# A transformer layer rewritten as one program, interleaved by batch

## The reference

```python
mod = (_silu(L0_c) @ L0_wmod).reshape(L0_c.shape[0], 6, 1, -1)
sa, ca, ga, sb, cb, gb = (mod[:, 0], ..., mod[:, 5])
ga = (2 * (ga >= 0) - 1) * jnp.maximum(jnp.abs(ga), 0.25)   # gb likewise
h = _layernorm(x, axis=-1) * (1 + ca) + sa
x = x + ga * _L0_attn_ref(h, ...)
h = _layernorm(x, axis=-1) * (1 + cb) + sb
x = x + gb * _L0_ffn_ref(h, ...)
```

## Time and profile before

| | us |
|---|---|
| median of three runs | 2005.65 |
| lowest, highest | 1998.06, 2006.18 |
| the profiled execution | 2002.72 |
| its span in the trace | 2000.9 |
| PE, DVE, ACT, POOL busy in the span | 1893.9, 1251.0, 1113.4, 486.1 |
| granted clock, mean | 0.967 |

### The profile page before, as it was taken

One profiled execution on the slowest core, in us unless ns is written; L12 is line 12 of the kernel. 1 busy time (PEld: TensorE's weight loads), 2 busy tenths in 40 slices (PEclk: granted clock), 3 DMA queues, 4 the chain that ended last, 5 costly groups with the idle time before them and its releaser, 6 DMA issues. The chain is left out here.

```text
span 2000.9 us, 30064 instructions
## 1 busy us (share of the span) xinstructions
PE 1893.9 (95%) x9271; PEld 1575.8 (79%) x9271; DVE 1251.0 (63%) x2969; ACT 1113.4 (56%) x2582; POOL 486.1 (24%) x466
## 2 busy tenths in 40 slices
PE   7769589999999999999999999999999967999999
PEld 3557278888888888888888888888888856788887
DVE  5864856666666766666676666666666636643534
ACT  3344356666666666666566666666656625523423
POOL 0620643324132240313413123131221111010010
PEclk8669789999999999999999999999999978999999
DMA  9100245655656555465654545546454455211010
GB/s 363 44 1 1 84 141 157 192 165 169 186 154 189 154 164 158 145 203 180 207 162 152 178 123 170 157 147 181 118 176 134 145 160 164 80 53 53 16 58 21
DMA packets 170380, 275.30 MB, mean 138 GB/s; under 512 B 18744, under 2 KB 111928, under 8 KB 170304
## 3 DMA queue, kind: packets, MB, share of 16 engines
q1 hardware_dynamic: 167760, 270.18, 43.7%
q10 hardware_dynamic: 2544, 4.19, 0.7%
HBM read 173.65 MB, written 100.66 MB: 137 GB/s over the span
## 5 line engine op out<-in xcount | busy, mean ns | idle before, releaser
L1526 DVE CUSTOM_DVE_ANT_0 ps<-ps,mask 128x512 f32<-128x512 f32 (+3 forms) x512 | 236.2, 522 | 339.2 <-PE ps L1250 339.0
L1211 PE MATMUL ps<-hA,wq 128*128 128x512 f32 x1536 | 386.0, 400 | 0.9 <-DVE qT L1511 0.8
L1283 PE MATMUL ps<-wo,oT 128*128 128x512 f32 x1536 | 372.8, 394 | 3.0 <-issue 1.6
L1416 ACT ACTIVATE pt<-pd 128x1280 fp32r<-128x1280 f32 x128 | 163.2, 1275 | 353.4 <-PE ps L1265 340.4
L1283 PEld LDWEIGHTS ps<-wo,oT 128*128 128x128 f32 x1536 | 287.9, 189 | 62.6 <-issue 1.8
L1211 PEld LDWEIGHTS ps<-hA,wq 128*128 128x128 f32 x1536 | 279.0, 188 | 57.9 <-issue 0.9
L1397 ACT ACTIVATE probs<-ps,nmax 128x512 f32<-128x512 f32 (+3 forms) x512 | 262.8, 532 | 47.9 <-DVE nmax L1526 47.9
L1265 PE MATMUL ps<-pt,V 128*128 128x512 f32 (+2 forms) x1152 | 252.9, 349 | 18.3 <-DVE pt L1550 18.3
L1405 ACT ACTIVATE probs<-probs,rinv 128x512 f32<-128x512 f32 (+3 forms) x512 | 246.2, 552 | 31.3 <-DVE rinv L1532 31.3
L1265 PEld LDWEIGHTS ps<-pt,V 128*128 128x128 f32 x1152 | 196.8, 190 | 45.7 <-issue 21.2
L1250 PE MATMUL ps<-kT,qT 128*128 128x512 f32 (+2 forms) x1152 | 225.3, 340 | 0.0
(11 more groups left out here) (205 smaller groups left out, 2623.6 us busy)
## 6 DMA issues: line engine op xcount, KB each, us to landing
turned_blocks<-tp SPq DMA_DIRECT2D x128, 640.0 KB, 2.9
pd<-turned_blocks SPq DMA_DIRECT2D x512, 160.0 KB, 3.3
wq_in<-in_L_attn_w_q_dram SPq DMA_DIRECT2D x16, 1024.0 KB, 6.3
wo_in<-in_L_attn_w_o_dram SPq DMA_DIRECT2D x16, 1024.0 KB, 7.1
wm<-in_L_wmod_dram SPq DMA_DIRECT2D x3, 2048.0 KB, 12.6
X<-in_L_attn_x_dram SPq DMA_DIRECT2D x4, 1024.0 KB, 10.7
wm_a<-in_L_wmod_dram SPq DMA_DIRECT2D x2, 2048.0 KB, 22.1
wk_in<-in_L_attn_w_k_dram SPq DMA_DIRECT2D x16, 256.0 KB, 3.9
```

The lines of the kernel that those rows point to most:

```text
L1211: last = nc.tensor.matmul(ps[:, bank, :], w[i][:, c, cols], hT[k][:, c, b * S:(b + 1) * S], start=(c == 0 and n == 0), stop=(c == DC - 1 a ...
L1283: last = nc.tensor.matmul(ps[:, bank, :], oT[x_][:, b, h, r * P:(r + 1) * P], wo[y_][:, h, :], start=(h == 0 and n == 0), stop=(h == GQ - ...
L1416: nc.scalar.activation(flat(pt[0][:]), flat(pd[:, u % 2]), ACT.Copy).then_inc(phi_done, 1)
L1526: nc.vector.tensor_tensor_reduce(out=v, in0=v, in1=mask[:, TB * P - KEYS[i]:], scale=-1.0, scalar=3e38, op0=ALU.add, op1=ALU.min, accum_ou ...
```

## The change

The two blocks become one, a single program for each engine with batches interleaved: attention of a later batch stands between pieces of the feed-forward of an earlier one. All twelve modulation vectors are made in it, and their weights go through three slots of two vectors each. Normalising for attention moves from DVE to ACT. The update of X by attention is a matmul: o_t is transposed once a batch, and 16 of its rows times G (the gate row, zero outside a head's 32 columns, made by transposing `spread`) give a PSUM tile that DVE adds to X. The rounded split of hT2 (low2) and of hA (low_2) moves from DVE to POOL. The choice of columns comes in last: DVE forms dense = dense * qsel * gate + X ahead, and at the end copies it into X where the choice, still in PSUM, is not zero (copy_predicated). In the third block the finish of the last modulations goes, and with it a wait.

```diff
-            def make_mod(pe, m, banks, wm):
-                    last = nc.tensor.matmul(ps[0:B, banks + m % 2, :], cT[:, MODS[m][0], k, :], wm[:, k, :],
-                                            start=(k == 0), stop=(k == DC - 1))
-                    last = nc.tensor.transpose(turned[:, k:k + B], mrow[:, m % 2, c * P:(c + 1) * P], ident[0:B, 0:B])
-                mods_finish(link, 1, turned_late, MOD_GA, 6, tmp_late)
-                dve.sem_inc(mods_done, 1)
+            QB = P // TB
+            cT = sb(l0, "cT", [P, 2, DC, QB], F32)
+            same_row = sb(l0, "same_row", [P, QB], F32)
+            NSLOT = 3
+            BANK_P, BANK_U, BANK_M, BANK_D = 2, 3, 5, 6
+            JOBS = [(1, 0), (1, 1), (1, 2), (2, 0), (1, 3), (2, 1), (2, 2), (2, 3), (3, 0), (3, 1)]
+            def bank_of(k):
+                if k < DC:
+                    return (0, 1, BANK_U, BANK_U + 1)[k]
+                return k % 2 + (BANK_U if k >= DC * (len(JOBS) - 2) else 0)
...
+                @block.sync
+                    def load_wm(k):
+                        if k >= NSLOT:
+                            sp.wait_ge(rows_full, 2 * (k - NSLOT) + 2)
...
+                    load_x(0)
+                    load_wm(0)
...
+                    load_x(1)
...
+                    load_wm(1)
+                    load_x(2)
+                    load_wm(2)
+                    load_x(3)
...
+                    for k in range(NSLOT, len(MODS) // 2):
+                        load_wm(k)
+                    load_kv(sp, 0)
...
+                @block.gpsimd
+                    pool.wait_ge(mods_done, 2)
+                    for b in range(B):
+                        gate = mod[0][:, DC * MOD_GA:DC * MOD_GA + DC, b:b + 1].to_broadcast([P, DC, P])
+                        nc.gpsimd.tensor_tensor(spread[:, b], place[:].rearrange("p c t e -> p c (t e)"), gate, ALU.mult) \
+                            .then_inc(spread_done, 1)
...
+                        for c in range(DC):
+                            pool.wait_ge(taken, chunk(2, b, c) + 1)
+                            nc.gpsimd.tensor_tensor(hP[b % 2][:, 1, c, :], hT2[:, c, :], hP[b % 2][:, 0, c, :].bitcast(F32),
+                                                    ALU.subtract).then_inc(low2, 1)
...
+                @block.scalar
+                    def normal1(b):
+                        act.wait_ge(inv1, b + 1)
...
+                            last = nc.scalar.activation(xh1[:, t % TB, :], X[:, t, :], ACT.Identity, bias=shift[:, t:t + 1],
+                                                        scale=rstd1[:, t:t + 1])
...
+                    root1(0)
+                    normal1(0)
+                    copy_mod(0)
+                    copy_mod(1)
+                    modulated1(0)
+                    root1(1)
+                    normal1(1)
+                    copy_mod(2)
+                    copy_mod(3)
+                    modulated1(1)
+                    exponentials(0)
+                    copy_mod(4)
+                    copy_mod(5)
+                    root1(2)
+                    normal1(2)
...
+                    for k in range(B):
+                        copy_rows(k)
+                    copy_o(0)
+                    copy_mod(6)
+                    copy_mod(7)
+                    modulated1(2)
+                    root1(3)
+                    root2(0)
+                    normal1(3)
...
+                        nc.scalar.activation(wf[:, c, :], ps[:, BANK_U + (c + 1) % 2, :], ACT.Copy).then_inc(wf_done, 1)
+                        nc.scalar.activation(wT[0][:, c, :], ps[:, BANK_U + (c + 1) % 2, :], ACT.Copy).then_inc(w_hi, 1)
+                    copy_mod(8)
+                    copy_mod(9)
+                    exponentials(1)
+                    modulated2(0)
+                    copy_mod(10)
+                    copy_mod(11)
+                    copy_o(1)
+                    modulated1(3)
+                    root2(1)
+                    for k in range(B, 2 * B):
+                        copy_rows(k)
+                    drain(0)
+                    drain(1)
+                    drain(2)
+                    exponentials(2)
+                    drain(3)
+                    modulated2(1)
+                    copy_o(2)
+                    clusters(0)
+                    root2(2)
+                    drain(4)
+                    drain(5)
+                    drain(6)
+                    drain(7)
+                    exponentials(3)
+                    modulated2(2)
+                    copy_o(3)
+                    clusters(1)
+                    root2(3)
+                    drain(8)
+                    drain(9)
+                    clusters(2)
+                    modulated2(3)
+                    drain(10)
+                    drain(11)
+                    clusters(3)
+                    for t in range(TB * (B - 1), NT):
+                        drain(t)
...
+                @block.vector
+                    def add_outputs(b):
+                            nc.vector.tensor_tensor(X[:, t, :], X[:, t, :], ps[:, BANK_U + t % 2, :], ALU.add).then_inc(x1_done, 1)
+                    def with_dense(b):
...
+                            last = nc.vector.scalar_tensor_tensor(dense[:, t, :], dense[:, t, :], qsel[:, t:t + 1], gb_rows[:, b, :],
+                                                                  ALU.mult, ALU.mult)
+                        link(last)
+                        for t in range(TB * b, TB * (b + 1)):
+                            last = nc.vector.tensor_tensor(dense[:, t, :], dense[:, t, :], X[:, t, :], ALU.add)
+                        link(last)
...
+                    scores(1)
+                    normal2(0)
+                    outputs(1)
+                    dve.wait_ge(mods_ps, len(MODS))
+                    mods_finish(link, 1, turned_mods[1], MOD_SA, 6, tmp_g)
+                    dve.sem_inc(mods_done, 1)
+                    add_outputs(1)
+                    statistics2(1)
+                    scores(2)
+                    normal2(1)
+                    outputs(2)
+                    cluster_logits(0)
+                    add_outputs(2)
+                    cluster_hits(0)
+                    statistics2(2)
+                    scores(3)
+                    normal2(2)
+                    outputs(3)
+                    cluster_logits(1)
+                    add_outputs(3)
+                    cluster_hits(1)
+                    statistics2(3)
+                    with_dense(0)
+                    normal2(3)
+                    cluster_logits(2)
+                    with_dense(1)
+                    cluster_hits(2)
+                    with_dense(2)
+                    cluster_logits(3)
+                    cluster_hits(3)
...
+                    with_dense(3)
+                    dve.wait_ge(chosen, ROWS_SPREAD)
+                    def select_rows(b):
+                            nc.vector.copy_predicated(X[:, t, :], ps[:, BANK_P, :].bitcast(I32), dense[:, t, :]).then_inc(x2_done, 1)
...
+                    select_rows(0)
+                    statistics(mv_2, 0, TB, var_2)
+                    select_rows(1)
+                    inverse_2(0)
+                    statistics(mv_2, TB, 2 * TB, var_2)
+                    select_rows(2)
+                    inverse_2(1)
+                    select_rows(3)
+                    statistics(mv_2, 2 * TB, NT, var_2)
...
+                @block.tensor
+                    def make_mod(m):
+                        cols = slice((m % 2) * D, (m % 2 + 1) * D)
+                        for k in range(DC):
+                            last = nc.tensor.matmul(ps[QB * k:QB * (k + 1), BANK_D + m % 2, :], cT[:, layer, k, :],
+                                                    wms[m // 2 % NSLOT][:, k, cols], start=True, stop=True)
+                    def turn_mod(m):
+                            last = nc.tensor.matmul(turned_mods[layer][:, k:k + B], mrow[:, m % 2, c * P:(c + 1) * P],
+                                                    same_row[:, 0:B], start=True, stop=True)
+                    def update(b, tiles):
+                            at = slice(QB * t, QB * t + E0)
+                            nc.tensor.matmul(ps[:, BANK_U + t % 2, :], oT_[at, :], G[at, b, :], start=True, stop=True).then_inc(upd_ps, 1)
...
+                    make_mod(2)
+                    make_mod(3)
+                    pe.wait_ge(mods_done, 1)
+                    turn_mod(2)
+                    turn_mod(3)
+                    pe.wait_ge(wcat_done, 2)
+                    project(0)
+                    turn(1, 1)
...
+                    dots(0)
...
+                    linear(0)
+                    linear(1)
+                    project(3)
+                    linear(2)
+                    linear(3)
+                    turn(2, 1)
...
+                    update(2, range(2))
+                    dots(1)
+                    update(2, range(2, TB))
+                    linear(4)
```

(39 more changed lines are left out.)

1071 lines of the change are left out of this document (488 added, 583 removed).

## The result

The changed kernel took 2024.66 us (median of 6 runs, 2018.37 to 2026.46) where the kernel before took 2004.52 beside it (6 runs, 1998.06 to 2006.18): a ratio of 1.0097, 95% interval 1.0076 to 1.0119. Slower was forecast, and the time lies within the range; the step from the kernel before was forecast at 11.2 us and came out near 20. The profiled execution took 2025.64 for a span of 2023.9. The second layer starts at 271.2 on ScalarE where it started at 249.5: 21.7 later. All that follows took 1752.7, against 1751.4. So nearly the whole difference lies in the first layer, and nearly all of what was mis-sized lies in one of its stages.

A forecast was written before the change was run, and what follows sets the result against it. The first layer, ending at 249.2 us, was the one place where no engine is full. Its stages summed to 260.4, so +11.2 on the profiled 2002.72 gave 2014 us; the 8-in-10 range was 1986 to 2028.

The forecast's parts named there:

- Stage D: linear(0) to linear(15): PE starts at 120.9, 84 us of work and 22 of waits, ending at 227.2.
- 22 us of waits: PE's waits between linear(0) and linear(15), from exponentials, copies and normalising queued behind other work; together 22 us.
- Stages A to C: Start through first projection, first update and scores(2): project(0) at 37.4, first update done 69.9, scores(2) done 121.5.
- a pair of vectors: Modulation matmuls in four column groups: 4.5 us a pair, the middle between 7.2 (no overlap) and 1.8 (all at once).
- stage C: From first update to scores(2): an ACT chain while DVE waits, exp(1) done at 95.1, scores(2) at 121.5.
- Stage E: Tail after the last linear: selection, statistics, normalising and modulating, to 260.4; 33 us against 44.9 before.
- the predicated copy: DVE's copy into X under a PSUM mask: 0.69 us each, eight on the path; bounds 480 and 1375 ns.
- The table load: ACT's table switches, ten: 1.28 us each, next activation at its end, without the skill's 1380 ns drain.
- Slower still: Rival: column groups do not overlap (13 us), predicated copy costs 1375 ns (5.5 us); 2032 us, chance 0.13.
- Cold start gone: Rival, first 110 us: four groups at once (14 us) and full clock from the second projection (12); 1988 us, chance 0.18.
- No change: Rival: half of the stalls between linear(0) and linear(15) (11 us) hide; 2003 us, chance 0.20.
- DVE the bound: Rival: interleaving makes DVE bound the first layer, ending at 188; 1942 us, chance 0.07.

The follow-up runs named there:

- e8: e2 with dummy 256-column matmuls in TensorE's waits ahead of the cluster products dots(1) and dots(2); 1997.54 us, ratio 0.9970 to the kernel before.
- e1: Changed kernel with 108 dummy 256-column matmuls in TensorE's waits of the linear stretch; 2010.70 us, ratio 1.0046 to the kernel before.
- e2: Changed kernel with the same instructions in another order in the linear stretch; 2002.28 us, ratio 1.0008 to the kernel before.
- e4: Changed kernel, tail alone: inverse_2(0) ahead of select_rows(1), second batch normalised by VectorE instead of ScalarE; 2023.64 us, ratio 1.0099 to the kernel before.
- e3: Changed kernel with column groups undone: a modulation vector's four matmuls accumulate in one group; 2045.49 us, ratio 1.0214 to the kernel before.
- e12: e8 with 56 dummy 128-column matmuls in the waits of the first 100 us; run twice, 1989.94 and 1989.51 us, ratios 0.9932 and 0.9930.
- e13: e12 with 19 more dummies in the last waits and the tail of e9; 1995.67 us, ratio 0.9962 to the kernel before.
- e7: e2 with turns and modulations of batches 1, 2 and 3 one step earlier; 1999.06 us, ratio 0.9972 to the kernel before.
- e9: e2 with batch 1's turns around linear(1), linear(7) ahead of dots(2), and a reordered tail, no dummies; 1996.59 us, ratio 0.9966.
- e6: e2 with 144 dummy 128-column matmuls among the narrow ones of project, dots and turned vectors; 2027.47 us, ratio 1.0102 to the kernel before.
- e11: e2 with project's operands exchanged: 48 stationary and 512 moving columns, copied and transposed back; 2005.42 us, ratio 1.0009 to the kernel before.
- e14: e13 with two 128-column dummies between the tiles of each project; 1995.24 us, ratio 0.9961 to the kernel before.

## Why the prediction was right in sign and wrong in size

**Stage D, "84 us" of PE's work at full clock: the step that failed.** The term was sized from a stretch in which PE never rests, and put beside 22 us of waits in the same sum. The records do take 79.4 at full clock (e8), so nothing was missing from the list, which was 4.6 too dear; but with the waits in it the clock was 0.78 and they took 102.8. Mis-sized by 18.8. The waits came out 8.1 shorter: 22 forecast, 13.9 measured, since a slower PE lets ScalarE and VectorE catch up; with the clock held in the same order (e1) the real work took 83.3 and the rest 23.2. Together 10.7, where the block's growth was missed by 10.5 (21.7 for 11.2). So the sum was right for a clock that the waits in it did not leave. The row that should have warned stood in the prediction: the attention at a clock of 0.78 with a projection at 6.52.

**The mechanism of the waits: right.** exp(2) behind drain(2), copy_o(2) behind modulated2(1), exp(3) behind drain(7), normal2(3) behind with_dense(0): each stands in the trace, and moving them (e2) took 21.5 us off the stretch, 7.6 of them idle time and 13.9 of them clock.

**Stages A to C: right in sum by luck, two errors of opposite sign.** project(0) started 3.1 early (34.3, not 37.4), and exp(1) ended at 87.9, not 95.1, in part because a pair of vectors cost 2.75 to 3.64 and not 4.5. Then dots(0) took 6.93 at half clock and the gate rows 3.7, which stage C had not listed as work of PE, and linear(0) started at 121.2 (118.9 and 116.2 in e1 and e4, with the same code ahead). The Trainium skill (TensorE: Matmul & The Clock Gate, Part 3: Packing small matmuls) has groups of width 32 at 1/2.38 of the time; here a pair is 7.05 in one group (e3) and 1.92 in four (e12), both at full clock: 3.7. The middle between "none" and "all" was the wrong choice: the Trainium skill's factor, 3.0 for a pair, was nearer, and the trace goes past it.

**Stage E: right,** 33.3 for 33.2, and so, nearly, were DVE's total, POOL's and the predicated copy. It hid one thing that e4 showed: the output statistics are 4 to 5 us from being last.

**The table load:** 1.28 and the exponential at once (load at 137.33, exponential at 138.62) as in the earlier trace rows. The Trainium skill (ScalarE: Activation LUTs, What ACT_TABLE_LOAD costs) adds a drain for each switch; the trace disagrees again.

**The rivals.** "Slower still" named the right side for the wrong reason: both its prices came out low. "Cold start gone" had a gain from four groups at once, which came, and a full clock, which did not: 0.62. "No change" rightly had idle time smaller than the list of stalls, but half clock took more than that back. "DVE the bound" was not reached in any run. Of the signs, VectorE's idle time was 3.9 ahead of the sums behind exp(1) (8 forecast) and 20.5 behind exp(2) (15), and the last linear ended at 237.9 (227).

What stays open: A2. Idle time as a trigger is shown in the linear stretch: by the order alone (e2) and by filling (e1, e8). Before it, e12 and e13 point the same way, less clearly. That narrow work draws the clock down by itself rests on falls with no pause ahead (project(1) in e3, linear(2) in the kernel after, in e7, e9 and e12's second run), and e6, e11 and e14 do not settle it; nor does anything here say why one execution falls and its twin does not.

## What to carry to other kernels

Where TensorE waits again and again, as here, price a wait twice: its length, and half clock for some of the work behind it; a sum that adds idle time to work priced at full clock can come out too low. An order that interleaves phases is worth what its queues allow: look for the small instruction (an exponential, a copy of 128 columns) that stands behind work which waits for something else, and move that first. Where a wait can't go, cheap matmuls in it can shorten the kernel (e1, e8, e12), but one wait taken out shows the next one in the queue, so look at the trace after each.

## What was not expected of the hardware

- 108 dummy matmuls, 16.8 us of TensorE's work, made the stretch that they stand in 10.2 us shorter and took the kernel from 1.0097 to 1.0046 of the one before (e1).
- Four column groups ran a pair of vectors in 1.92 us where one group takes 7.05.
- Four predicated copies of 128x512 with the mask in PSUM take 2.54 us, and 2.59 with GpSimd busy beside them (at 257.29).
- Four additions of 128x512 on VectorE take 2.50 us, and 6.71 beside GpSimd's subtractions (at 211.67).
- With the same instructions the linear stretch took 88.0 and 91.4 us in two executions, by one fall of the granted clock for some 7 us (e12).
